# Four layers of cross-attention on one core: values of four streams in three tiles, an fp32 output product, rounds written out, new instruction orders

## The reference, cut to what matters

```python
def gqa(x, cond, wq, wk, wv, wo, norm_w):          # 16 heads of 8, 4 key/value heads
    xn = x * rsqrt(mean(x * x) + 1e-5) * norm_w
    q, k, v = xn @ wq, cond @ wk, cond @ wv
    attn = softmax(q k^T / sqrt(8))                # 128 queries, 77 keys
    return x + (attn @ v) @ wo

def mha(x, ctx, mask_A, mask_B, Wq, Wk, Wv, Wo, bo, tokens_A, tokens_B):   # 16 heads of 64
    q, k, v = x @ Wq, ctx @ Wk, ctx @ Wv           # Wv: 256 x 1024
    logits = q k^T / 8
    logits[:, :, tokens_A] += -20 * (1 - mask_A)   # likewise tokens_B with mask_B
    return x + (softmax(logits) @ v) @ Wo + bo
```

## Time and profile before

| | |
|---|---|
| three runs | 1964.11, 1966.53, 1967.25 us |
| the profiled execution | 1973.73 us, its span 1971.9 us |
| granted TensorE clock | 0.969 |
| busy: PE, PEld, DVE | 1882.1, 1578.3, 1677.6 us |
| busy: ACT, POOL | 1453.1, 1496.9 us |
| instructions | 76204 |

### The profile page before, as it was taken

One profiled execution on the slowest core, in us unless ns is written; L12 is line 12 of the kernel. 1 busy time (PEld: TensorE's weight loads), 2 busy tenths in 40 slices (PEclk: granted clock), 3 DMA queues, 4 the chain that ended last, 5 costly groups with the idle time before them and its releaser, 6 DMA issues.

```text
span 1971.9 us, 76204 instructions
## 1 busy us (share of the span) xinstructions
PE 1882.1 (95%) x28656; PEld 1578.3 (80%) x28784; DVE 1677.6 (85%) x3516; ACT 1453.1 (74%) x2603; POOL 1496.9 (76%) x1830
## 2 busy tenths in 40 slices
PE   5599999999999999999999999999999999999996
PEld 5478888888788887888788887888878888888884
DVE  7588888898788987888888988889878898888883
ACT  4377777777777776777777777777767777777772
POOL 2478888788787877788777887878878888888872
PEclk7599999999999999999999999999999999999997
DMA  5279999999899998899979997999989999999985
GB/s 160 50 126 167 162 168 167 169 160 163 155 174 167 159 168 150 168 162 161 168 150 169 159 166 145 175 169 160 165 150 176 163 163 163 159 152 170 160 158 107
DMA packets 1164823, 310.79 MB, mean 158 GB/s; under 512 B 1139254, under 2 KB 1163132, under 8 KB 1164412
## 3 DMA queue, kind: packets, MB, share of 16 engines
q1 hardware_dynamic: 1164412, 305.43, 88.1%
HBM read 15.93 MB, written 4.19 MB: 10 GB/s over the span
## 4 chain that ended last, share of the span: by engine, by line
PE 81%; DMA 5%; issue 3%; DVE 3%; SPq 3%; POOL 2%; ACT 2%; ACTq 0%; DVEq 0%
PE ring L1135 46%; PE sc L1268 9%; PE o_ps L1135 8%; DMA arena<-p_sm 5%; PE o_ps L1286 4%; PE ring L1337 4%; PE sc L1251 3%; PE sc L1266 2%; POOL arena L589 1%; PE ring L1206 1%; POOL p_sm L566 1%; ACT arena L627 1%; PE ring L1318 1%; PE ring L1334 1%; PE sc L1243 1%
## 5 line engine op out<-in xcount | busy, mean ns | idle before, releaser
L561 POOL TENSOR_TENSOR p_sg<-arena,p_sg 128x512 f16<-128x512 f32 (+1 forms) x256 | 347.4, 1357 | 216.1 <-ACT p_sg L627 216.1
L1135 PE MATMUL ring<-ctx_two,m_w 128*128 128x154 f16 x6144 | 447.1, 233 | 0.0
L1135 PEld LDWEIGHTS ring<-ctx_two,m_w 128*128 128x128 f16 x6144 | 433.7, 99 | 1.0 <-DVE o_tg L821 0.9
L1004 DVE TENSOR_TENSOR arena<-sc,row_max 128x616 f32<-128x616 f32 (+2 forms) x512 | 405.2, 792 | 4.5
L566 POOL TENSOR_TENSOR p_sm<-arena,p_sm 128x616 f16<-128x616 f32 x256 | 336.8, 1316 | 46.9 <-ACT p_sm L627 46.9
L1135 PE MATMUL ring<-wv_m,ctx_two 128*77 128x512 f16 x1536 | 365.5, 383 | 0.1
L627 ACT ACTIVATE arena<-ring 128x462 f16<-128x462 f32 (+1 forms) x384 | 196.3, 512 | 136.9 <-PE ring L1135 136.9
L589 POOL TENSOR_TENSOR arena<-arena 128x1024 f16<-128x1024 f32 x128 | 273.1, 2133 | 30.2 <-ACT arena L627 19.1
L1135 PEld LDWEIGHTS ring<-wv_m,ctx_two 128*77 128x77 f16 x1536 | 166.0, 117 | 149.9 <-DVE q_mix L825 46.1
L1001 DVE TENSOR_REDUCE row_max<-sc 128x6 f32<-128x462 f32 (+2 forms) x384 | 223.7, 582 | 55.6 <-PE sc L1268 55.5
L1268 PE MATMUL sc<-arena,x_s 128*128 128x512 f16 (+1 forms) x1152 | 262.5, 337 | 7.0
(11 more groups left out here) (160 smaller groups left out, 3529.9 us busy)
## 6 DMA issues: line engine op xcount, KB each, us to landing
ctx_nat<-in_ctx_dram SPq DMA_DIRECT2D x64, 77.0 KB
x_nat<-in_x_dram SPq DMA_DIRECT2D x64, 64.0 KB, 2.2
arena<-p_sg SPq DMA_TRANSPOSE x256, 4.2
arena<-p_sm SPq DMA_TRANSPOSE x256, 3.9
out_dram<-y_out SPq DMA_DIRECT2D x64, 64.0 KB, 2.0
arena<-in_L_xattn_Wk_dram SPq DMA_DIRECT2D x2, 1024.0 KB, 6.0
arena<-in_L_xattn_Wv_dram SPq DMA_DIRECT2D x2, 1024.0 KB, 6.7
arena<-arena SPq DMA_TRANSPOSE x128, 5.8
```

What stands on the lines that cost most here:

```text
L561: pool.tensor_tensor(p_sg[k][:, LO, 0:e - a], probs_flat[:, a:e], p_sg[k][:, HI, 0:e - a], ALU.subtract).then_inc(sems["pg_lo"], 1)
L1004: dve.tensor_tensor(shifted[:, hs, :], s_view[:, hs, :], row_max[:, hs].unsqueeze(2).to_broadcast([P, hs.stop - hs.start, S]), ALU.subtrac ...
L1135: ins = pe.matmul(out, a, b, start=(n == 0), stop=(n == len(passes) - 1))
```

## The change

1. *Values of four streams in three tiles.* The context of four streams lies in one tensor, `ctx_four`, in which each stream has 77 + 26 columns. POOL copies a third of the fourth stream's columns behind each of the other three (`context_parts`). Their value products then have 103, 103 and 102 output rows, and the fourth stream has none of its own. Its rows are moved by DMA from the three tiles into a tile of its own (`move_values`). The pairs make 2, 1, 2 and 1 chunks (`value_chunks`).
2. *GQA output product in fp32.* `wo_g` and `o_tg` are one fp32 tensor each; DVE's `low_turned` is gone.
3. *All rounds written out*, on all five engines.
4. *All orders set anew*, the ring's too. Some stages move to the next pair (`rest_and_turn`, `turn_out`, the second `turn_m`, DVE's second `normalise_m`, POOL's `low_out`) or to the pair before (`x_parts` of g, `last_layer`, `turned`).

```diff
+    PART = -(-S // 3)
+    PART_OF = [(i * PART, min(S, (i + 1) * PART)) for i in range(3)]
+    def part(m):
+        return stream(m) % 4
+    def rows(m):
+        a, e = PART_OF[part(m)]
+        return S + e - a
+    def tile_of(m):
+        return ((m - PLACES[1]) // 2 % PAIRS // 4 * 3 + part(m)) % 2 if part(m) != 3 else 2
+    def value_chunks(n):
+        m = 2 * n + 1
+        return {0: [(m, 1), (m + 2, 0)], 1: [(m, 1)], 2: [(m, 0), (m, 1)], 3: [(m + 2, 0)]}[part(m)]
...
-        return [("g", lead, chunks[0]), ("g", lead, chunks[1]), ("g", lead, chunks[2]), ("ym", m - 6, 0), ("ct", g + 4, 0),
-                ("vp", g, 0), ("yg", g - 4, 0), ("kv", g + 2, 0), ("q", g + 2, 0), ("ot", g - 2, 0),
-                ("v", m, 0), ("v", m, 1)]
+        return [("ot", g - 4, 0), ("ym", m - 6, 0), ("g", lead, chunks[0]), ("g", lead, chunks[1]), *[("ct", g + 4, 0)] * (layer(g + 4) == 0 or n % PAIRS == CT_EXTRA),
+                ("g", lead, chunks[2]), ("kv", g + 2, 0), *[("v", j, k) for j, k in value_chunks(n)[0:1]], ("vp", g, 0), ("q", g + 2, 0),
+                ("yg", g - 4, 0), *[("v", j, k) for j, k in value_chunks(n)[1:2]]]
...
-        wo_g = [sb(f"wo_g{n}", [P, 2, D], F16) for n in range(2)]
+        wo_g = [sb(f"wo_g{n}", [P, D], F32) for n in range(2)]
...
-        ctx_two = [sb(f"ctx_two{n}", [P, 2, KC, 2, S], F16) for n in range(STREAMS // 2)]
-        ctx_t = [ctx_two[n // 2][:, :, :, n % 2, :] for n in range(STREAMS)]
+        ctx_four = [sb(f"ctx_four{n}", [P, 2, KC, 4, S + PART], F16) for n in range(STREAMS // 4)]
+        ctx_t = [ctx_four[n // 4][:, :, :, n % 4, 0:S] for n in range(STREAMS)]
...
-        v_mha = [sb(f"v_mha{n}", [P, 2, H, MD + 1], F16) for n in range(2)]
+        v_tile = [sb(f"v_tile{n}", [P, 2, H, MD + 1], F16) for n in range(2)]
+        v_fourth = sb("v_fourth", [P, 2, H, MD + 1], F16)
+        v_mha = v_tile + [v_fourth]
...
+            def move_values(it, m):
+                a, e = PART_OF[part(m)]
+                sp.wait_ge(sems["v_lo"], at("v_lo", it, m, 2))
+                sp.nop(nofuse=True)
+                fourth = m - 2 * (part(m) + 1)
+                if exists(it, fourth):
+                    sp.wait_ge(sems["om_raw"], at("om_raw", it, fourth, 2))
+                    sp.nop(nofuse=True)
+                moved = m - (2 if part(m) else 4)
+                if exists(it, moved):
+                    sp.wait_ge(sems["v_moved"], at("v_moved", it, moved, 16))
+                    sp.nop(nofuse=True)
+                sp.dma_start(v_fourth[a:e].rearrange("p a h d -> p (a h d)"),
+                             v_mha[tile_of(m)][S:S + e - a].rearrange("p a h d -> p (a h d)")).then_inc(sems["v_moved"], 16)
...
             def pair(it, n):                       # SP
+                if exists(it, m - 2):
+                    turn_m(it, m - 2, 1)
+                if exists(it, m - 2) and part(m - 2) != 3:
+                    move_values(it, m - 2)
+                if exists(it, m - 4):
+                    turn_out(it, m - 4)
                 if exists(it, g):
                     turn_g(it, g, 0)
                     turn_g(it, g, 1)
+                if exists(it, m):
+                    turn_m(it, m, 0)
...
-                if exists(it, m):
-                    turn_m(it, m, 0)
-                    turn_m(it, m, 1)
-                if exists(it, m - 2):
-                    turn_out(it, m - 2)
...
-            with sp.Fori(1, NIT - 2) as it:
+            for it in range(1, NIT):
...
+            def context_parts(it, g):
+                c = ctx_four[stream(g) // 4]
+                pool.wait_ge(sems["ct_lo"], at("ct_lo", it, g, 1))
+                for n, (a, e) in enumerate(PART_OF):
+                    piece = c[:, :, :, 3, a:e].rearrange("p a k s -> p (a k) s")
+                    ins = pool.tensor_tensor(c[:, :, :, n, S:S + e - a].rearrange("p a k s -> p (a k) s"), piece,
+                                             ones_h[:, :].unsqueeze(2).to_broadcast([P, 2 * KC, e - a]), ALU.mult)
+                ins.then_inc(sems["ct_parts"], 1)
...
             def values(it, n, m, k):               # ACT
-                if k == 0 and exists(it, m - 4):
-                    act.wait_ge(sems["om_raw"], at("om_raw", it, m - 4, 2))
+                before, r = same_tile_before(m), rows(m)
+                if k == 0 and exists(it, before):
+                    act.wait_ge(sems["om_raw"], at("om_raw", it, before, 2))
+                    act.wait_ge(sems["v_moved"], at("v_moved", it, before, 16))
...
             def context_values(it, n, m, k):       # PE
+                w, b, (n0, n1), r = layer(m) // 2, bank_for(it, n, ("v", m, k)), V_CHUNKS[k], rows(m)
+                ct = ctx_four[stream(m) // 4][:, :, :, part(m), :]
+                if k == 0:
+                    pe.wait_ge(sems["ct_parts"], at("ct_parts", it, split_stream(m), 1))
+                split_product(ring[0:r, b, :],
+                              [(hl(lambda i: ct[:, i, kc, 0:r]), hl(lambda i: wv_m[w][:, i, kc, n0:n1])) for kc in range(KC)]).then_inc(sems["v_raw"], 1)
...
             def output_g(it, n, g):
-                pe.wait_ge(sems["ot_lo"], at("ot_lo", it, g, 1))
-                split_product(ring[:, b, 0:T], [(hl(lambda i: wo_g[w][:, i, :]), hl(lambda i: o_tg[:, i, :]))]).then_inc(sems["yg_raw"], 1)
+                pe.wait_ge(sems["ot_copy"], at("ot_copy", it, g, 1))
+                pe.matmul(ring[:, b, 0:T], wo_g[w][:, :], o_tg[:, :], start=True, stop=True).then_inc(sems["yg_raw"], 1)
```

More of the change, by code:

```diff
@@ L121, in build @@
         "turned_m0": times(16, m_each), "turned_m1": times(16, m_each),
-        "v_raw": times(2, m_each), "v_hi": times(2, m_each), "v_lo": times(2, m_each),
+        "v_raw": times(2, m_each), "v_hi": times(2, m_each), "v_lo": times(2, m_each), "v_moved": times(16, m_each),
         "om_raw": times(2, m_each), "om_rcp": times(2, m_each), "om_norm": times(2, m_each),
@@ L128, in build, with counts @@
     BY_TWO = ("g_raw", "g_hi", "g_lo")
+    THREE_OF_FOUR = ("v_raw", "v_hi", "v_lo", "v_moved")
+    def counts(name, n):
+        st, la, _ = ITEMS[n]
+        if (name in BY_TWO and st % 2) or (name in THREE_OF_FOUR and st % 4 == 3) or (name == "ct_parts" and st % 4 != 3):
+            return 0
+        return PER_ITEM[name][la]
     def at(name, it, j, k):
-        per = [PER_ITEM[name][ITEMS[n][1]] * (name not in BY_TWO or ITEMS[n][0] % 2 == 0) for n in range(SLOTS)]
+        per = [counts(name, n) for n in range(SLOTS)]
         late = [per[n] * ITEMS[n][2] for n in range(SLOTS)]
@@ L614, in _ @@
                 pair(0, n)
-            with pool.Fori(1, NIT - 1) as it:
+            for it in range(1, NIT):
                 for n in range(PAIRS):
                     pair(it, n)
-            for n in range(PAIRS):
-                pair(NIT - 1, n)
             for n in range(TAIL):
@@ L758, in high_turned @@
                     act.wait_ge(sems["yg_raw"], at("yg_raw", it, g - 2, 1))
-                high(o_tg[:, HI, :], ring[:, b, 0:T], 1.0).then_inc(sems["ot_hi"], 1)
+                high(o_tg[:, :], ring[:, b, 0:T], 1.0).then_inc(sems["ot_copy"], 1)
             def last_layer(it, n, m):
@@ L772, in pair @@
                     folded(it, n, lead, chunks[1])
-                    folded(it, n, lead, chunks[2])
+                if layer(g + 4) == 0 and exists(it, g + 4):
+                    turn_context(it, n, g + 4)
                 if exists(it, g):
@@ L776, in pair @@
                     high_g(it, g, 0)
-                if layer(g + 4) == 0 and exists(it, g + 4):
-                    turn_context(it, n, g + 4)
+                if exists(it, lead):
+                    folded(it, n, lead, chunks[2])
+                if exists(it, g + 2):
+                    keys_values(it, n, g + 2)
                 if exists(it, g):
                     exponential_g(it, g, 1)
-                if layer(m - 6) == LAYERS - 1 and exists(it, m - 6):
-                    last_layer(it, n, m - 6)
-                if exists(it, g):
                     high_g(it, g, 1)
+                for j, k in value_chunks(n)[0:1]:
+                    if exists(it, j):
+                        values(it, n, j, k)
                 if exists(it, g + 2):
-                    keys_values(it, n, g + 2)
+                    queries(it, n, g + 2)
                 if exists(it, g):
@@ L1109, in pair @@
                 if exists(it, m):
[L1110 removed]
                     shift_m(it, m, 1)
[L1112 to L1116 removed]
+                if exists(it, g - 4):
+                    finish_g(it, n, g - 4)
+                if exists(it, m - 2):
+                    normalise_m(it, n + 1, m - 2, 0)
+                for j, k in value_chunks(n)[1:2]:
+                    if exists(it, j):
+                        values(it, n, j, k)
             for n in range(-3, PAIRS):
                 pair(0, n)
[L1120 removed]
+            for it in range(1, NIT):
                 for n in range(PAIRS):
                     pair(it, n)
```

(5 more changed lines are left out.)

187 lines of the change are left out of this document (90 added, 97 removed).

## The result

The changed kernel takes 1936.15 us (median of four runs, 1933.31 to 1939.14), against 1965.45 us (1964.11 to 1967.25) for the kernel before: a ratio of 0.985, 95% interval 0.983 to 0.987. That is 29 us faster where 102 were forecast, and 71 us above the forecast of 1865. The profiled execution has a span of 1934.6 us and a granted clock of 0.973.

The account below looks back on a forecast made before the run. It took PE's full queue as the bound: 1973.7 - 82 (value matmuls) + 13 (fp32 product) - 30 - 3 (written-out rounds) = 1871.7, less 7.2 for the profiled run: 1865 us, chance 0.64, range 1840 (1847 likelier) to 1908.

Parts of the forecast that it names:

- Value matmuls: On PE, 1152 value matmuls instead of 1536, 384 fewer at 0.213 us each: -82 us, wider weight loads staying covered.
- The fp32 product: GQA output product on PE: one fp32 product of 0.26 us replaces three fp16 passes of 0.16, +13 us (-3 to +35).
- Written-out rounds: Five loop back-edges lose PE's idle and slow clock, 5 x 5.9 = -30 us, and pairs shorten, -3 us.
- Rival B: Stalls at rounds stay, because fetching code as such stalls: 1898 us, chance 0.06.
- Orders: New orders on all engines cost 0, with thin cover in pairs holding one value chunk.
- Added work: `context_parts` on POOL stays hidden; the 96 `move_values` transfers and three waits on SP cost 0, 192 us if each awaited.
- Rival C: DMA transfers bound the pairs at 14.9 us and it gets slower, +192 to 2057 us; chance 0.04.
- Rival D: Dealing saves nothing, since the fourth stream waits for its moved rows each time: +70, 1935 us; chance 0.06.
- Rival A: Cover too thin: the 64 one-chunk pairs each miss by 0.6 us in waits between engines, +38, 1903 us; chance 0.2.
- a mean pair over 14.2 us: Sign in the measured pairs that would prove the forecast wrong; PE's pair starts were to alternate near 12.75 and 14.0 us.

Follow-up runs that it names:

- experiment 1: Kernel before, with each of its 640 DMA transposes replaced by a plain copy of as many bytes in 256-byte pieces: 1972.56 us, 1.003.
- experiment 3: Kernel before with plain copies for transposes (experiment 1), its loop rounds written out on all engines: 1947.8 us, 0.990.
- with copies: Stand-in with the 640 DMA transposes as plain copies of as many bytes, same waits: kernel before 1972.56 us, changed kernel 1867.99 us.
- Experiments 9 to 11: experiment 9, Experiment 10, and the kernel before with copies, those of the MHA probabilities in 128-byte pieces: the last 2033.91 us, 1.035.
- Experiment 7: Changed kernel with plain copies for transposes, each copy issued as three DMAs of a third, same bytes and pieces: 1915.39 us, 0.974.
- Experiment 10: Changed kernel with plain copies for transposes, only the 256 copies of MHA probabilities in 128-byte pieces: 1994.42 us, 1.014.
- experiment 2: Changed kernel with its 640 DMA transposes replaced by plain copies of as many bytes in 256-byte pieces: 1867.99 us, 0.950.
- stand-ins: Changed kernel with copies, moves issued by ACT: 1981.84 us with the 128-byte pieces of Experiment 10, 1890.75 us with the copies in three of Experiment 7.
- experiment 9: Changed kernel with plain copies for transposes, every copy in 128-byte pieces instead of 256, twice as many: 2262.16 us, 1.149.

## Why the prediction was wrong

*Value matmuls, 384 x 0.213 = -82.* Right in kind and size. The group has 1152 matmuls at 0.243 us of busy time each, as against 0.238 in the earlier trace rows, the stationary side's load grew from 117 to 127 ns and stayed covered (PE idle for 0.2 us in this group), and the dealing was worth 77.9 us with room in the queue.

```profile
L1205 PE MATMUL ring<-wv_m,ctx_four 128*103 128x512 f16 (+1 forms) x1152 | 280.1, 379 | 0.2
...
L1205 PEld LDWEIGHTS ring<-wv_m,ctx_four 128*103 128x103 f16 (+1 forms) x1152 | 145.0, 127 | 95.1 <-ACT v_all L702 0.3
```

*The fp32 product, +13.* Measured 8.9 by itself, within its bounds of -3 and +35. On PE's row it is 18: each product stands 0.30 us before its successor, and not the 0.26 that I had taken from `L1334`. The Trainium skill (FP8 and Floating Point Precision, TensorE Precision Notes) counts four passes for it, which I had made an estimate of +7 from. The time of the run lies between that and the row's 13; the trace has 0.304 us against 0.165 for three fp16 passes, more than four to three.

*Written-out rounds, -33.* Measured -24.8. The idle went as priced. The slow clock was priced too high, because I took the one back-edge that I had looked at closely for all five: 3.1 us each, where experiment 1 shows 0.1 to 3.1. The pairs behind the back-edges of the kernel before say the same, 16.43, 17.45, 17.67, 16.26 and 17.61 us. Rival B did not come: the pairs of experiment 3 that are longer wait for a DMA, and the loop has them too.

*Orders, 0.* About -11 us with copies (-20 by the other count), the one term that I had no row for.

*Added work, `move_values`: cost 0, and each transpose lands some 3 us before PE needs it.* This is the step that failed, and 68 of the 71 us go with it. I checked SP's list for one hold-up, the wait for `v_lo`, and found its semaphore set in time, which it was. I did not add up the list. SP's list in a pair with inputs was five transposes, two loads and a store, and then the new move; a turn of it came to 15.04 us, in pairs that were at the same time to shrink to 13.3 and 14.6 us. By the mean issue times of the kernel before, with 1.2 us between the DMAs as in the timeline above, I would have found some 12.6 us (an estimate): 0.7 us to spare in the shorter of the two, so a warning and not yet the overrun. The slack stood in the trace of before, in a view that I did not read: SP's own waits, 473 us, or some 3.3 us a pair without those of the start. Moves take 0.6 us a pair from it (78 us over 1700), the shorter round 0.85 (233.2 less 219.6 us, over 16 pairs), and what the transposes' issues grow by 1.5 ((166 + 39 - 27 for the `turn_g`s) over 119 pairs): 3.0 of 3.3 on the mean, and more than there is in the first eight pairs of a round, which had 1.7 each before (13.8/8). Half of the 3.0 is the growth of the transposes' own issues, which no row of before foretold, and whose cause is open. PE then waits for the tightest of the transposes. `turn_out` lands 5.4 us after its issue at the median, no later than before (5.8), but it is issued 4.0 us late, against the 3 us of cover that I had worked out.

*Rival C, 0.04.* Its mechanism comes nearest, and its price was wrong. I dismissed it because the DMA share had touched 1.19 in one stretch and so "counts packets that stand waiting". Experiments 9 to 11 show what that did not exclude: more time on the engines does cost time where their share over the whole run is near 100%, +61 for the kernel before at 98% and +126 for the one after at 102%. The changed kernel stands at 99.4%, the one before at 88.1%. C's 2.0 us for a move was too dear (0.83 on SP's queue). The 71 us are 0.55 us per pair, below the 0.79 from which C was to eat up the gain.

The Trainium skill (Perfetto Trace Analysis, What "DMA-bound" means) names these two among the limits of a kernel, the engines, and the sequencer of the engine that issues, seen as a track of solid DMA slices. The timeline of SP above is such a track; in pairs without inputs SP still waits, 10.6 us for `p_sm` from 620 to 732 us. Experiment 7 fills the second and leaves the first (67.8%). Experiment 10 fills the first (102.3%) and leaves SP 603 us of waits. Both give PE's waits for the output, and experiment 10 gives 31.5 us for probabilities besides.

*Rival D, 0.06, 1935 us.* It has the right number by chance. No wait for `v_fourth` is in PE's list, and dealing saves its 78 us where the queue has room. *Rival A* did not come: the pairs without inputs are 12.8 and 14.1 us where SP keeps up, and from 150 to 1850 us PE's list has no wait for DVE. The sign that I had named for a wrong forecast, a mean pair over 14.2 us, was set too high: by the starts the mean is 14.15 us (14.43 before, 13.61 in experiment 2).

*What stays open.* No run tells how the 68 us between experiment 2 and the changed kernel divide between SP's time and the engines' time. Experiment 7 has the changed kernel's issue time at 67.8% of the engines and loses 47; that leaves 21 us to the engines if the two add up, which nothing here shows. The transposes themselves were not varied, and one that takes SP 2.2 us may do so because the engines behind it are full: the shortest is 1.5 us in both kernels. The moves show that the engines' share alone doesn't set an issue time: 0.83 us at 99.4% in the changed kernel, 1.16 at 67.4% in experiment 2, 2.44 at 102.3% in experiment 10. Nor was a version of the changed kernel with its transposes and with the moves on ACT tried; by the stand-ins it would gain between 12.6 us (engines full) and 24.6 us (queue full).

## What to carry to other kernels

Where one engine issues all DMAs, write its list for a pair with issue times from the trace, add it up, and compare it with the length that the pair is to have after the change, not the one it has. The slack is the sum of that queue's own waits, read for the fullest pairs apart. Allow for issues that grow when the queue fills. A change that shortens the pair eats the slack too (10.9 us of experiment 7's 47), and DMAs that cost 5 us in a queue with slack cost 42 in one without. A DMA share of 88% is a number to be tested, not explained away: the kernel before lost 61 us at 98%.

## What the runs showed of the hardware that was not expected

- A DMA transpose of `p_sm` holds SP's queue for 1.5 us at the least, 1.6 (before) or 2.2 us (after) at the median and 3.8 or 3.7 at the most, where a plain copy of the same bytes in the same pieces holds it for 0.59. The instruction is the same in both kernels, so part of the time must come from what it meets there. A move shows the same, with medians from 0.83 to 2.44 us.
- A 256-byte piece takes an engine 23.8 ns (before) or 25.8 ns (after) in a transpose and 16.3 in a copy, by the mean over 1.1 million pieces (medians 18, 18 and 15). A piece of 128 bytes takes 19.4 ns in experiment 9, and 18.1 in experiment 10 beside 19.4 for one of 256, so the time goes by the number of pieces more than by bytes.
- The 16 engines' packet time can exceed the span (125.4% in experiment 9), so that 100% is no ceiling of this number.
- The clock need not fall alike after like idles: behind five idles of 2.5 to 3.0 us at the back-edges of experiment 1, the next pair took 3.1, 2.2, 0.1, 3.1 and 1.7 us more than its kind.
